# Down pass of a cross-attention and SwiGLU kernel: the weight codes asked for by SyncE behind the turned pieces, the result rows by GpSimd

## What is computed

```python
x = x + xattn(layernorm(x), ctx, Wq, bq, Wk, bk)
# feed forward, with 4-bit codes of type int32 and one scale for every 64 codes
W = NF4_CODE[q.reshape(-1)].reshape(-1, 64) * absmax[:, None]      # gate, up, down
g = einsum('bsh,mh->bsm', layernorm(x), Wg)
u = einsum('bsh,mh->bsm', layernorm(x), Wu)
out = x + einsum('bsm,hm->bsh', silu(g) * u, Wd)
```

## Time and profile before

| | |
|---|---|
| median of three runs | 1919.1 us |
| the profiled execution, its own time | 1918.35 us |
| span of its trace | 1916.2 us |
| mean granted TensorE clock | 0.999 |
| TensorE busy | 1898.2 us, 99% |
| VectorE busy | 1623.0 us, 85% |
| ScalarE busy | 1448.2 us, 76% |
| GpSimd busy | 370.3 us, 19% |
| hardware queue (SyncE's DMAs) | 393280 packets, 170.55 MB, 39.6% of 16 engines' span |
| software queue (GpSimd's DMAs) | 44032 packets, 153.65 MB, 25.0% |
| chain that ended last | TensorE 72%, ScalarE 12%, VectorE 8%, issue 4% |

### The profile page before, as it was taken

The page is one execution under the profiler, slowest core; times in us unless marked ns, Lnnn a source line. Parts: engine busy times, 40 slices in busy tenths (PEclk is TensorE's granted clock), DMA queues, the critical chain, the costliest instruction groups (busy, mean ns, idle before and its releaser), DMA issues.

```text
span 1916.2 us, 29499 instructions
## 1 busy us (share of the span) xinstructions
PE 1898.2 (99%) x9758; PEld 963.7 (50%) x9758; DVE 1623.0 (85%) x2694; ACT 1448.2 (76%) x2697; POOL 370.3 (19%) x568
## 2 busy tenths in 40 slices
PE   9999999999999999999999999999999999999999
PEld 4487888744444444444444444444444444444444
DVE  7978999869889899899898888898798898896963
ACT  3887776588998988988988988988999999900000
POOL 2023353301111121121121121121123222210110
PEclk9999999999999999999999999999999999999999
DMA  9338999955554565454454454465679988974462
GB/s 356 71 85 189 259 262 276 309 156 130 118 145 125 119 152 130 114 153 130 113 153 126 112 157 120 114 159 134 143 192 225 249 228 217 229 254 131 156 234 84
DMA packets 437640, 326.14 MB, mean 170 GB/s; under 512 B 371680, under 2 KB 371952, under 8 KB 435568
## 3 DMA queue, kind: packets, MB, share of 16 engines
q1 hardware_dynamic: 393280, 170.55, 39.6%
q0 software_dynamic: 44032, 153.65, 25.0%
q10 hardware_dynamic: 176, 0.07, 0.0%
HBM read 154.31 MB, written 82.31 MB: 123 GB/s over the span
## 4 chain that ended last, share of the span: by engine, by line
PE 72%; ACT 12%; DVE 8%; issue 4%; DMA 0%; SPq 0%; DVEq 0%; POOL 0%; ACTq 0%
PE ps L2294 39%; PE ps L2337 23%; PE ps L1682 7%; ACT sq L347 4%; ACT sq L343 3%; PE ps L1650 2%; PE ps L1717 2%; DVE w L363 1%; DVE tail L2447 1%; ACT halves L415 1%; ACT tail L2368 1%; ACT w L347 1%; ACT w L343 1%; ACT tail L2383 1%; DVE halves L431 1%
## 5 line engine op out<-in xcount | busy, mean ns | idle before, releaser
L2294 PE MATMUL ps<-T,wS 128*128 128x512 f16 x4704 | 1017.7, 379 | 5.1 <-DVE ps L2402 2.5
L2294 PEld LDWEIGHTS ps<-T,wS 128*128 128x128 f16 x4704 | 459.6, 98 | 560.0 <-issue 6.7
L347 ACT ACTIVATE sq<-sq 128x512 f32<-128x512 f32 x898 | 516.9, 628 | 0.0
L363 DVE SCALAR_TENSOR_TENSOR w<-sq,w 128x512 f32<-128x512 f32 x590 | 415.9, 705 | 117.0 <-ACT sq L347 107.7
L343 ACT ACTIVATE sq<-q 128x512 f32<-128x512 int32 x598 | 363.9, 632 | 49.1 <-DVE w L363 48.6
L2337 PE MATMUL ps<-T,tail 128*128 128x512 f16 x1584 | 346.7, 380 | 3.9 <-DVE tail L2489 2.7
L2337 PEld LDWEIGHTS ps<-T,tail 128*128 128x128 f16 x1584 | 155.2, 98 | 192.8 <-issue 5.8
L431 DVE SCALAR_TENSOR_TENSOR halves<-w,halves 128x512 f16<-128x512 f32 x240 | 163.0, 688 | 6.4 <-ACT halves L415 6.1
L2337 PE MATMUL ps<-T,wS 128*128 128x512 f16 x768 | 168.4, 379 | 0.0
L2242 POOL DMA_DIRECT2D keep_h<-tail x196 | 106.2, 542 | 292.0 <-DVE tail L2447 291.7
L415 ACT CAST halves<-w 128x512 f16<-128x512 f32 x204 | 126.7, 622 | 43.2 <-DVE w L363 31.6
(11 more groups left out here) (244 smaller groups left out, 1868.6 us busy)
## 6 DMA issues: line engine op xcount, KB each, us to landing
keep_h<-tail POOLq DMA_DIRECT2D x196, 256.0 KB, 2.5
tail<-keep_h POOLq DMA_DIRECT2D x66, 512.0 KB, 4.9
wS<-keep_h POOLq DMA_DIRECT2D x32, 512.0 KB, 4.9
q<-in_L_ffn_down_q POOLq DMA_DIRECT2D x56, 256.0 KB, 4.2
T<-in_x SPq DMA_DIRECT2D x13, 1024.0 KB, 8.6
q<-in_L_ffn_up_q POOLq DMA_DIRECT2D x52, 256.0 KB, 3.0
q<-in_L_ffn_gate_q POOLq DMA_DIRECT2D x48, 256.0 KB, 3.5
keep_x<-T SPq DMA_DIRECT2D x38, 256.0 KB, 4.2
```

Of the source, the lines that this page charges most:

```text
L347: nc.scalar.activation(place, place, ACT.Square, bias=b, scale=a).then_inc(un.s_act, 1)
L363: nc.vector.scalar_tensor_tensor(out=out, in0=square_place(un, u, i - 1), scalar=FACTORS[i - 1][1], in1=un.w[:, buf, :], op0=ALU.add, op1= ...
L2294: last = nc.tensor.matmul(ps[:, bank, :], un.wS[:, z % SLOTS, a, kt, :], t.Tp[side][product][:, :, b, kt, :], start=fresh and n == 0, stop ...
```

## The change

In the down pass SyncE asks for the codes of a phase right after it has issued the turns of that phase, and no longer three steps ahead; GpSimd issues the rows' stores, the partial sums' loads and the residual's loads, at the same c (the stores one c earlier), behind the `load_h` of the step. The eight stores of the last group stay with SyncE. Loads 9 to 55 count on the first set of semaphores again. In the weights' sums one semaphore takes the place of two, with the same instructions.

```diff
@@ loaded_at
     if u < PLAN.early_loads:
         return un.s_q[u % Q_RING], ring_count(u, Q_RING)
-    return un.s_qp[u % Q_RING], ring_count(u - PLAN.early_loads, Q_RING)
+    if u < PLAN.late_loads:
+        return un.s_qp[u % Q_RING], ring_count(u - PLAN.early_loads, Q_RING)
+    mine = [n for n in range(u + 1) if n % Q_RING == u % Q_RING and (n < PLAN.early_loads or n >= PLAN.late_loads)]
+    return un.s_q[u % Q_RING], 16 * len(mine)
@@ Plan
+        self.late_loads = Q_RING + sum(len(us) for phase, us in self.loads.items() if phase < DOWN_PHASE)
@@ feed_forward, sync
         for m in range(DOWN_STEPS):
-            group, c = m // CH_PAIRS, m % CH_PAIRS
             turns_due(DOWN_PHASE + m)
-            if group == 1 and c == 0:
-                sp.wait_ge(s_v, 2 * STAGES)
-                sp.wait_ge(t.s_store, 16 * BATCH)
-                for i in range(HST_RING):
-                    sp.wait_ge(s_hst[i], 16 * (FORMS // HST_RING))
-            for j in range(BANKS):
-                if group > 1 and c == (ROWS_AT + j if group in KEPT_GROUPS else ROWS_AT):
-                    store_y(group - 1, j)
-            for j in range(BANKS):
-                if group in PART_OF and c == Y_AT:
-                    load_part(group, j)
-            for j in range(BANKS):
-                if group in ROW_GROUPS and c == (Y_AT + j if group == 1 else Y_AT):
-                    load_y(group, j)
+            for u in PLAN.loads.get(DOWN_PHASE + m, ()):
+                load_unit(nc, sp, un, t, u)
         for j in range(BANKS):
-            store_y(PRODUCTS - 1, j)
-        for i in range(2):
-            sp.wait_ge(s_st[i], 16 * BANKS * 3)
+            tile, cols = out_place(PRODUCTS - 1, j)
+            sp.wait_ge(s_yev, BANKS * (PRODUCTS - 1) + j + 1)
+            sp.dma_start(t.out_t[:, tile, cols], t.y_out_rows[j]).then_inc(s_end, 16)
+        sp.wait_ge(s_end, 16 * BANKS)
+        sp.wait_ge(s_st[0], 16 * BANKS * 2)
+        sp.wait_ge(s_st[1], 16 * BANKS * 3)
@@ feed_forward, gpsimd
         for m in range(DOWN_STEPS):
-            for ahead in range(Q_AHEAD) if m == 0 else (Q_AHEAD - 1,):
+            group, c = m // CH_PAIRS, m % CH_PAIRS
+            for ahead in range(FORMS_AHEAD) if m == 0 else (FORMS_AHEAD - 1,):
                 if m + ahead < CH_PAIRS:
                     stores_due(SLOT_COUNT + m + ahead)
-                if m == 0:
-                    loads_due(DOWN_PHASE + ahead)
             load_h(m + H_RING)
-            loads_due(DOWN_PHASE + m + Q_AHEAD)
+            if group == 1 and c == 0:
+                pool.wait_ge(s_v, 2 * STAGES)
+                pool.wait_ge(t.s_store, 16 * BATCH)
+                for i in range(HST_RING):
+                    pool.wait_ge(s_hst[i], 16 * (FORMS // HST_RING))
+            for j in range(BANKS):
+                if group > 1 and c == (ROWS_AT + j if group in KEPT_GROUPS else ROWS_AT) - 1:
+                    store_y(pool, group - 1, j)
+            for j in range(BANKS):
+                if group in PART_OF and c == Y_AT:
+                    load_part(pool, group, j)
+            for j in range(BANKS):
+                if group in ROW_GROUPS and c == (Y_AT + j if group == 1 else Y_AT):
+                    load_y(pool, group, j)
```

More of the change, by code:

```diff
@@ L2113, in feed_forward @@
     FORMS_BY_CLEAR = max(m for m, bank in enumerate(LATE_BANKS) if bank == Y + 1) + 1
-    Q_AHEAD, ROWS_AT, Y_AT = 3, 1, 3
+    FORMS_AHEAD, ROWS_AT, Y_AT = 3, 1, 3
     BANKS = 8
@@ L2128, in feed_forward @@
         sem(n) for n in ("s_xy", "s_p5", "s_z", "s_v", "s_silu", "s_h", "s_hsum", "s_hhi", "s_hlo", "s_hd", "s_dn", "s_yev"))
-    s_wdif, s_wsum, s_wsumhi, s_wsumlo, s_pre, s_part = (
-        sem(n) for n in ("s_wdif", "s_wsum", "s_wsumhi", "s_wsumlo", "s_pre", "s_part"))
+    s_wdif, s_wsumhi, s_wsumlo, s_pre, s_part, s_end = (
+        sem(n) for n in ("s_wdif", "s_wsumhi", "s_wsumlo", "s_pre", "s_part", "s_end"))
     def evicted(stage, product, side):
@@ L2182, in turns_due @@
                 turn_piece(nc, sp, un, t, z)
[L2184 to L2203, removed]
         for k in range(SLOT_COUNT):
@@ new lines, in sync, with load_y @@
+        for j in range(BANKS):
+            tile, cols = out_place(PRODUCTS - 1, j)
[4 more added lines that the diff above has]
+        sp.wait_ge(s_st[1], 16 * BANKS * 3)
+    def load_y(queue, group, j):
+        tile, cols = out_place(group, j)
+        if group > 1:
+            rows_stored(queue, group - 1)
+        queue.dma_start(t.y_out_rows[j], t.ys[:, tile, cols]).then_inc(s_yl[ROW_GROUPS.index(group) % 2], 16)
@@ new lines, in load_part, with store_y @@
+    def load_part(queue, group, j):
+        kept = PART_OF[group]
+        rows_stored(queue, kept)
+        if group == 4:
+            queue.wait_ge(un.s_wlo, GATE_UP_PIECES + DOWN_UNITS)
+        else:
+            queue.wait_ge(s_pre, BANKS * PRE_GROUPS.index(4) + j + 1)
+        queue.dma_start(t.part[j], t.yp[KEPT_GROUPS.index(kept), :, j, :]).then_inc(s_part, 16)
+    def store_y(queue, group, j):
+        tile, cols = out_place(group, j)
+        queue.wait_ge(s_yev, BANKS * group + j + 1)
+        dst = t.yp[KEPT_GROUPS.index(group), :, j, :] if group in KEPT_GROUPS else t.out_t[:, tile, cols]
+        queue.dma_start(dst, t.y_out_rows[j]).then_inc(s_st[group % 2], 16)
@@ L2462, in sum_of @@
             nc.vector.tensor_tensor(tmp, left[:, 0], right[:, 0], ALU.subtract).then_inc(s_wdif, 1)
[L2463 removed]
+            dve.wait_ge(s_wdif, 3 * n + 1)
             nc.vector.tensor_tensor(tmp, tmp, left[:, 1], ALU.add).then_inc(s_wdif, 1)
[L2465 to L2466 removed]
+            dve.wait_ge(s_wdif, 3 * n + 2)
+            nc.vector.tensor_tensor(tmp, tmp, right[:, 1], ALU.subtract).then_inc(s_wdif, 1)
             used = (3 * CH_PAIRS + pair, pair, CH_PAIRS + pair)[which]
             dve.wait_ge(*down_freed(used))
[L2469 removed]
+            dve.wait_ge(s_wdif, 3 * n + 3)
             nc.vector.tensor_copy(place[:, 0], tmp).then_inc(s_wsumhi, 1)
```

2 lines of the change are left out of this document (removed).

## The result

| | before | after |
|---|---|---|
| median of six runs, us | 1918.58 (1917.31 to 1922.13) | 1935.32 (1931.76 to 1940.02) |
| profiled execution: time, span, us | 1918.35, 1916.2 | 1935.28, 1933.1 |
| ratio to before, 95% interval | | 1.0083, 1.0071 to 1.0096 |

A forecast was written before the change was run, and what follows sets the result against it. ScalarE's squares were taken to pace the down pass, VectorE and TensorE following. A 6.4 us ScalarE shift plus 1.7 us of half clock made 8.1 on 1918.35: 1926.5, said as 1927 us; range 1922.5 to 1934.

The forecast's parts named there:

- What bounds: Down pass: ScalarE's squares pace decoding, VectorE follows, TensorE waits at group ends; ScalarE's waits are never made up.
- The margins: Code loads on SyncE: time from load start to ScalarE's need, 5.1 us inside groups, 1.3 at unit 21.
- Part 1: Code loads behind SyncE's turns, the deciding term: ScalarE shifted 0.3 + 2.6 + 3.5 = 6.4 us when group 2 ends.
- Medians of 3.5 to 4.8 fit. I take 0, with 0 to 2 us in all: Loads away from group ends: median landings fit the 5.1 us available, so no cost, 0 to 2 us for the upper end.
- one middle landing (3.9, 4.3) for each end: Loads 21 and 35, where groups 0 and 1 end: landings of 3.9 and 4.3 us make them 2.6 and 3.5 late.
- Part 2: Rows through GpSimd: cost 0; load_h has 26 us of cover against 19, parts and rows are used eight steps later.
- waits of 3, 1.0 and 5.5 us: TensorE's waits for VectorE's evictions at the ends of groups 0, 1 and 2, in that order.
- The clock's 1.7 us: TensorE after its wait where group 2 ends: half clock adds 1.7 us, range 0 to 3.4.
- the small loss: Rival: loads take 3.1 us and no clock drop follows; 4.1 us lost, 1922.4 to 1923 us; chance 0.24.
- The single queue as the pace: Rival: loads of 6.1 us behind turns miss the 5.1 us in every unit; about 1940 us; chance 0.07.
- The faster case: Rival: GpSimd freed of waits, VectorE reaches the first eviction 2.7 us sooner; 1913.5 us; chance 0.05.
- My proof of it: SyncE's queue: landing of 3.5 us with 1.3 us head start shows a turn done before the load behind it.

The follow-up runs named there:

- e5: Changed kernel with the four code loads of units 21, 22, 35 and 36 asked for ahead of their turns, the others behind; 1929.34 us, ratio 1.0042.
- e3: Against the kernel before, only the code loads move to SyncE, behind the turns; the rows stay with SyncE, behind the loads; 1928.44 us, ratio 1.0051.
- e4: Against the kernel before, only the rows move to GpSimd; GpSimd still asks for the codes, three units ahead; 1927.56 us, ratio 1.0043.
- e6: Changed kernel with rows of groups 1 to 3 issued by SyncE and those from group 4 by GpSimd, loads behind turns; 1930.26 us, ratio 1.0045.
- e1: Changed kernel with SyncE asking for the codes of each phase ahead of the turns, rows on GpSimd; 1918.9 us, ratio 1.0014.
- e13: Changed kernel with SyncE asking for the codes ahead of the turns and the rows left with SyncE; 1919.54 us, ratio 1.0000.
- e11: Kernel before, with GpSimd's code loads of units 16 to 50 also waiting for the low half of the unit three before; 1936.33 us, ratio 1.0097.
- e2: Changed kernel with codes read in runs of 2 KB rather than 512 B, so other weights land; 1932.35 us, ratio 1.0073.

## Why the prediction was right in sign and half in size

- **What bounds** held: ScalarE without slack, VectorE behind it, TensorE at the ends of groups. Every wait of ScalarE up to the end of group 2 came through to TensorE, and the earlier trace rows was the row that said so.
- **The margins** of Part 1 held to a tenth: 5.1 us inside groups, 1.3 said and 1.4 found at unit 21, 0.8 and 0.9 at unit 35. Turns issued in 1.24 us, the load 1.3 us behind them. "The next units have at least a microsecond more each" held as well, but the third unit behind an end has only 2.9 to 3.4 us (e5), less than many landings.
- **The step that failed** is the sizing of Part 1: "Medians of 3.5 to 4.8 fit. I take 0, with 0 to 2 us in all", and one middle landing (3.9, 4.3) for each end. The median was right, 4.4. But in a chain without slack each landing above its margin is paid, and one below it gives nothing back, so over 35 loads the tail sets the sum. The ends stayed within my bounds (4.8 and 6.0); the insides did not (0.8, or 2 at the most). Ends: 4.8 + 4.2 measured where I took 2.6 + 3.5 (landings 6.2 and 5.1). Inside: 2.2 + 1.6 + 0.4 where I took 0.3 in all. That is 13.3 us for 6.4, and it carries 6.9 of the 8.6 us missing between 8.1 and 16.7; 0.7 more are the 0.1 us that each stop costs beside its wait, and 0.6 were there before the decoding began. The earlier trace rows had maxima of 6.1, 6.8 and 5.8 on few samples each; all are above 5.1, and 35 draws were to come.
- **Part 2, "Cost 0"**, was wrong beside the loads: a loss of 16.7 us against 10.2 (e3) behind turns, and 9.4 us with the codes on GpSimd (e4). It was right on `load_h`, which was never late, though a burst of 16 took longer than 8.7 us (last section), and groups 4 to 6 stayed as long (e6), though VectorE waits there 12.3 us for rows that before came in time. It was wrong that rows have eight steps: group 1's are asked for one a step up to c = 10, and in e4 the last came 2.2 us late. What I left out besides is that transfers asked for by GpSimd need not wait for a turn and so run beside codes that now had no margin, and beside turns. That this is how the 6.5 us come about was not tried by itself: it stays open which of the rows, or which turns, make the landings longer.
- **TensorE**: waits of 3, 1.0 and 5.5 us were said, 5.1, 3.9 and 4.4 measured. At the first end 2.2 us of unit 16 arrived, which I had put at 0.3; the second got all of units 21 and 26. The clock's 1.7 us at the end of group 2 was right and counts once: the half-clock stretches at the first two ends, 2.9 and 2.4 us, are made up for, since TensorE waits for VectorE at the next end anyway.
- **The rivals**: the small loss needed loads of 3.1 us at the ends; they took 6.2 and 5.1. The single queue as the pace is out: 29 of 35 units don't wait by more than 0.1 us, and with the same queue e1 and e13 cost nothing. The faster case had nothing to act on, as said: ScalarE had no wait to lose, and VectorE reached the first eviction 2.9 us later and not sooner (1477.12 against 1474.22).
- **The Trainium skill**, "DMA: Bandwidth & Descriptors", "Queues, rings and completion order", says that one row's descriptors are consumed in ring order, and I let it speak against the change: the load pays for the turn ahead. The trace agrees in that all 35 loads land behind their turns. But in e1 each load still stands behind a turn and costs nothing, and in e11 none does and the loss is whole; so a turn ahead may lengthen a landing, but the loss doesn't need one. My proof of it was wrong: a landing of 3.5 us with 1.3 of head start comes ahead of the median turn of the earlier trace rows, 5.6, and not behind it. Those were turns of another stretch; the eight turns right ahead of the loads of the earlier trace rows landed in 3.2 to 4.8 us, and each load 0.7 to 3.2 us behind its turn. The shorter first byte of the SyncE path ("Specifications" of the same page of the Trainium skill) doesn't show: the medians are 4.4 and 4.3.

## What to carry to other kernels

Ask for a load on the event that frees its buffer, not behind a later event that happens to stand ahead in the same queue: what looks like a queue's cost was the lost lead of some 5 to 10 us. Where the consumer is busy 100% of a stretch, hold its margin against the longest of many landings, not the median, and walk through the loads one by one, adding each excess: a wait lengthens the margin of the next load, so the excesses don't simply add up. And when a transfer is moved to a queue that waits for less, ask what it will now run beside.

## What the runs showed of the hardware that I had not expected

The same code loads are other packets when SyncE asks for them. The page's packets, before, and with the loads alone moved (e3):

```profile
DMA packets 437640, 326.14 MB, mean 170 GB/s; under 512 B 371680, under 2 KB 371952, under 8 KB 435568
```

```profile
DMA packets 458695, 326.14 MB, mean 169 GB/s; under 512 B 371680, under 2 KB 396016, under 8 KB 456624
```

There are 24064 more under 2 KB: 47 loads of 512 packets of 512 B. From 2 to 8 KB there are 3008 fewer: 47 loads of 64 packets of 4 KB. So GpSimd's loads merge the runs of 512 B and SyncE's don't. What this is worth here e2, where SyncE reads runs of 2 KB, leaves between nothing and some microseconds.

GpSimd can stand in its own issue. Its burst of 16 row transfers in group 4, which I had put at 16 x 0.54 = 8.7 us, took 19.3 us:

```profile
1732.86 2.33 POOL L2218 DMA_DIRECT2D sq<-keep_p  x4
1735.18 1.06 POOL L2218 DMA_DIRECT2D w<-keep_p  x2
1736.87 0.54 POOL L2218 DMA_DIRECT2D w<-keep_p  x1 [0.62 <-issue]
1742.19 0.54 POOL L2218 DMA_DIRECT2D w<-keep_p  x1 [4.78 <-issue]
1742.72 3.18 POOL L2209 DMA_DIRECT2D tail<-keep_y  x6
1745.89 0.55 POOL L2209 DMA_DIRECT2D wS<-keep_y  x1
1751.63 0.54 POOL L2209 DMA_DIRECT2D wS<-keep_y  x1 [5.19 <-issue]
1752.16 2.10 POOL L2249 DMA_DIRECT2D tail<-keep_h  x4
```

After seven it waits 4.8 us for nothing that the profile shows, after the next eight 5.2. With `load_h`'s 26 us of cover this cost nothing; with 15, by my estimate from the 19.3 us, it would have.
